# Full 64-row stacks of the k and q parts in the DRAM scratch of an attention and feed-forward block

## What is computed

```python
xn = layernorm(x)                                   # x: (8, 1024, 256)
u, v, q, k = split(silu(xn @ W1 + b1), 4)
scores = einsum('bqhd,bkhd->bhqk', q, k)            # 16 heads of 16 features
av = einsum('bhqk,bkhd->bqhd', silu(scores) / S, v)
attn = (layernorm(av * u) * gamma + beta) @ W2 + b2
h = gelu((layernorm(xn) * g1 + b1') @ ternary(w1).T + fb1)
ffn = (layernorm(h) * g2 + b2') @ ternary(w2).T + fb2
out = x + attn + ffn
```

## Time and profile before

| | |
|---|---|
| median of 3 runs | 1576.9 us |
| the profiled execution | 1573.26 us |
| its span, first to last instruction | 1571.5 us |
| mean granted PE clock | 0.985 of full speed |
| PE busy | 1473.2 us, 94% |
| ACT busy | 1207.9 us, 77% |
| DVE busy | 897.5 us, 57% |
| DMA queue of SP | 121.81 MB in 62192 packets |
| HBM read, written | 79.84 MB, 41.94 MB |

### The profile page before, as it was taken

One profiled execution on the slowest core, in us unless ns is written; L12 is line 12 of the kernel. 1 busy time (PEld: TensorE's weight loads), 2 busy tenths in 40 slices (PEclk: granted clock), 3 DMA queues, 4 the chain that ended last, 5 costly groups with the idle time before them and its releaser, 6 DMA issues.

```text
span 1571.5 us, 25337 instructions
## 1 busy us (share of the span) xinstructions
PE 1473.2 (94%) x9826; PEld 779.0 (50%) x9826; DVE 897.5 (57%) x1716; ACT 1207.9 (77%) x1269; POOL 101.4 (6%) x193
## 2 busy tenths in 40 slices
PE   4599999999999999999989999999999999999987
PEld 3245454545545555454545545455454555545434
DVE  4447644576546754476545764467554676447544
ACT  1378787887878888687878888788787888868783
POOL 2000100001000100001000010000100010000000
PEclk9699999999999999999999999999999999999999
DMA  4623116430345204352063311653034610535100
GB/s 151 147 67 69 55 33 143 117 84 5 78 109 134 55 15 112 90 108 55 14 148 89 73 55 33 143 122 79 2 74 114 135 54 14 114 88 108 28 1 28
DMA packets 62312, 123.43 MB, mean 79 GB/s; under 512 B 7664, under 2 KB 9328, under 8 KB 61168
## 3 DMA queue, kind: packets, MB, share of 16 engines
q1 hardware_dynamic: 62192, 121.81, 32.8%
HBM read 79.84 MB, written 41.94 MB: 77 GB/s over the span
## 4 chain that ended last, share of the span: by engine, by line
issue 66%; PE 22%; POOLq 4%; ACT 2%; DVE 2%; DMA 2%; POOL 1%; DVEq 0%; SPq 0%; ACTq 0%
PE outs L949 8%; PE scores L930 5%; POOLq L524 2%; PE fill L986 2%; PE fill L1020 2%; PE fill L1004 2%; ACT attn L557 2%; PE fill L1036 1%; PE fill L1013 1%; DMA KS<-k_scratch 1%; DMA q_scratch<-qst 1%; POOLq L516 1%; POOL rs L510 1%; POOLq L500 1%; PE fill L995 0%
## 5 line engine op out<-in xcount | busy, mean ns | idle before, releaser
L557 ACT ACTIVATE attn<-scores 128x1024 f32<-128x1024 f32 x1024 | 991.0, 1024 | 257.6 <-PE scores L930 253.7
L949 PE MATMUL outs<-attn,V 128*32 128x512 f32 x4096 | 499.6, 606 | 0.0
L930 PE MATMUL scores<-QS,KS 64*128 64x512 f32 x2048 | 395.6, 455 | 48.5 <-DMA KS<-k_scratch 24.4
L930 PEld LDWEIGHTS scores<-QS,KS 64*128 64x128 f32 x2048 | 165.0, 186 | 346.1 <-ACT attn L557 258.6
L949 PEld LDWEIGHTS outs<-attn,V 128*32 128x32 f32 x4096 | 108.0, 110 | 242.0 <-issue 241.8
L820 DVE TENSOR_TENSOR tmp<-fill,l2g 128x512 f32<-128x512 f32 x128 | 88.5, 691 | 112.3 <-PE fill L1013 105.6
L803 DVE SCALAR_TENSOR_TENSOR hid<-fill,ratq,fb1b 128x512 f32<-128x512 f32 x128 | 96.1, 751 | 66.3 <-PE fill L1004 62.9
L1020 PE MATMUL fill<-Wq,hgh 128*128 128x256 f32 x512 | 131.9, 295 | 1.9 <-DVE hgl L827 1.1
L986 PE MATMUL fill<-xp,W1h 128*128 128x512 f32 x384 | 126.6, 411 | 0.8 <-ACT qst L563 0.8
L1020 PE MATMUL fill<-Wq,hgl 128*128 128x256 f32 x512 | 125.0, 282 | 0.0
L1020 PEld LDWEIGHTS fill<-Wq,hgh 128*128 128x128 f32 x512 | 97.4, 190 | 22.4 <-issue 16.1
(11 more groups left out here) (110 smaller groups left out, 1358.9 us busy)
## 6 DMA issues: line engine op xcount, KB each, us to landing
QS<-q_scratch SPq DMA_DIRECT2D x128, 256.0 KB, 7.6
k_scratch<-kst SPq DMA_DIRECT2D x64, 256.0 KB
q_scratch<-qst SPq DMA_DIRECT2D x64, 256.0 KB
KS<-k_scratch SPq DMA_DIRECT2D x64, 256.0 KB, 4.3
KS<-k_scratch SPq DMA_DIRECT2D x128, 128.0 KB, 5.2
xin<-in_x SPq DMA_DIRECT2D x8, 1024.0 KB, 8.2
out_dram<-part SPq DMA_DIRECT2D x16, 512.0 KB, 2.6
w1raw<-in_W SPq DMA_DIRECT2D x1, 1024.0 KB, 7.1
```

Source lines behind the costliest of these rows:

```text
L557: nc.scalar.activation(attn_of(g)[:, 2 * hf:2 * hf + 2, :], SP[:, 2 * hf:2 * hf + 2, :], ACT.Silu).then_inc(s_silu, 1)
L930: ins = mm(SP[:, j, :], KS[rows, pair, t * P:(t + 1) * P], QS[rows, pair - c * PPC, h * HALF:(h + 1) * HALF], start=True, stop=True)
L949: ins = mm(OP[32 * j:32 * j + 32, g // RUN % 2, :], V[:, t, c * HPC // 2 + j, o * DH:o * DH + 2 * DH], attn_of(g)[:, n, :], start=(o == 0 ...
```

## The change

The scratch tensors get 64 rows per head in place of 32. `write_parts` writes the high part and the rest twice each, in the order in which the stack wants them: four transfers for k and four for q in place of two and two. `load_k` and `load_q` then need one transfer of 64 rows for each e: two in place of six, and two in place of four. The bytes that are loaded stay the same. The bytes that are written to scratch double, from 33.6 MB (128 transfers of 256 KB) to 67.1 MB. No other engine's instructions change.

```diff
+K_ROWS = (0, 1, 1, 0)
+Q_ROWS = (0, 1, 0, 1)
-WROTE = 16 * PARTS
-K_STACKED = 16 * 6
-Q_STACKED = 16 * 4
+WROTE = 16 * len(K_ROWS)
+K_STACKED = 16 * 2
+Q_STACKED = 16 * 2
...
-    kd = [nc.dram_tensor(f"k_scratch{c}", [HPC, QROWS, SEQ], F32, kind="Internal").ap() for c in range(DC)]
-    qd = [nc.dram_tensor(f"q_scratch{c}", [HPC, QROWS, SEQ], F32, kind="Internal").ap() for c in range(DC)]
+    kd = [nc.dram_tensor(f"k_scratch{c}", [HPC, TERMS, SEQ], F32, kind="Internal").ap() for c in range(DC)]
+    qd = [nc.dram_tensor(f"q_scratch{c}", [HPC, TERMS, SEQ], F32, kind="Internal").ap() for c in range(DC)]
...
                 sp.wait_ge(s_split, 8 * b + n + 1)
-                for r in range(PARTS):
-                    sp.dma_start(kd[c][:, r * DH:(r + 1) * DH, cols], kst[:, r, :].bitcast(F32)).then_inc(s_kw, 16)
+                for r, part_of in enumerate(K_ROWS):
+                    sp.dma_start(kd[c][:, r * DH:(r + 1) * DH, cols], kst[:, part_of, :].bitcast(F32)).then_inc(s_kw, 16)
                 sp.wait_ge(s_split, 8 * b + n + 2)
-                for r in range(PARTS):
-                    sp.dma_start(qd[c][:, r * DH:(r + 1) * DH, cols], qst[:, r, :].bitcast(F32)).then_inc(s_qw, 16)
+                for r, part_of in enumerate(Q_ROWS):
+                    sp.dma_start(qd[c][:, r * DH:(r + 1) * DH, cols], qst[:, part_of, :].bitcast(F32)).then_inc(s_qw, 16)
...
                 for e in range(2):
-                    for at_row, first, rows in ((0, 0, QROWS), (QROWS, DH, DH), (QROWS + DH, 0, DH)):
-                        sp.dma_start(KS[e * TERMS + at_row:e * TERMS + at_row + rows, pairs, cols].bitcast(F32),
-                                     kv[e, first:first + rows, :, cols]).then_inc(s_kst[c][h], 16)
+                    sp.dma_start(KS[e * TERMS:(e + 1) * TERMS, pairs, cols].bitcast(F32),
+                                 kv[e, :, :, cols]).then_inc(s_kst[c][h], 16)
...
                 for e in range(2):
-                    for at_row in (0, QROWS):
-                        sp.dma_start(QS[e * TERMS + at_row:e * TERMS + at_row + QROWS, :, cols].bitcast(F32),
-                                     qv[e, :, :, cols]).then_inc(s_qst[h], 16)
+                    sp.dma_start(QS[e * TERMS:(e + 1) * TERMS, :, cols].bitcast(F32),
+                                 qv[e, :, :, cols]).then_inc(s_qst[h], 16)
```

## The result

The changed kernel takes 1641.7 us, the kernel before 1578.7 us on the same chip (medians of four runs each). The ratio is 1.0398 with a 95% interval of 1.0362 to 1.0434: 4.0% slower, 63 us. The forecast was 1615.5 us in a range of 1595 to 1648, with 0.85 on slower. The sign and the place were right; the size was not, 63 us in place of 39.

A forecast was written before the change was run, and what follows sets the result against it. PE was taken to bound the kernel, waiting at group 8 on a queue of transfer bytes. 2.6 - 1.7 + 5.2 - 2.0 = +4.1 us in eight bodies, 32.8, plus 5.8 for the clock, gave 1615.5 us, range 1595 to 1648.

The forecast's parts named there:

- writes of h=1: Queue between the h=0 loads and the wait of `load_k`: four 256 KB writes become eight, 5.2 us more per body.
- the door: PE's wait at the scores of group 8 for the second half of `KS`: from 3.05 to about 7.1 us.
- KS load of h=1: Last load before group 8: 1.0 MB at 225 GB/s takes 4.7 us in place of 6.7, 2.0 us less.
- rival 3: Loads get no faster, 192 GB/s stays because of a DRAM-side limit: 1645 to 1656 us, chance 0.09.
- two more q writes for h=0: Writes before SP's KS load of h=0: 1.3 us each, 2.6 us more per body, bounds 1.2 and 3.7.
- loads of h=0: KS and QS loads, 2.1 MB in 64-row transfers at 225 GB/s: 9.3 us in place of 11.0, 1.7 less.
- Nothing gives it back: After group 8: PE's later work follows in the same order, so the +4.1 us per body stays.
- The wait at group 0: Sign of being wrong: a new PE wait for QS of more than a few us; first body's first group 0.9 later.
- The clock: PE at the 1.2 GHz level after all eight group 8 waits: four more at 1.44 us, 5.8 us, bounds 0 and 17.
- c=1 at nothing: Writes and loads for c=1 grow by 8 us but have some 40 us of cover until group 40: no cost.
- Rival 1: Tall loads run at 353 GB/s like those over 128 partitions: -1.0 us per body, 1563 us, chance 0.10.
- Rival 2: Loads at 300 to 335 GB/s, gain and cost cancel: time stays at 1572 to 1582 us, chance 0.05.

The follow-up runs named there:

- the run with parts innermost: Changed kernel with the scratch reordered so the copies of a feature lie side by side, two copies per write, against the kernel before: ratio 0.9853, 1558.9 us.
- the changed kernel with 16 engines: Changed kernel with W1 and b1 columns reordered so a write's slowest DRAM dimension is 16 features, not 8 heads, against the kernel before: ratio 0.9961, 1574.7 us.

## Why the prediction was right, and where its size was off

*Place and mechanism: right.* The queue works in the order of issue, the writes of h=1 stand between the loads and the next load, and the door is group 8. The wait for KS was to be 57 us in eight times; it is 52.1 in eight, and 67.9 with the part of it that is taken at group 0. SP's KS load of h=1 was to be issued 13.6 us after the split of `q.0.1`; it is issued 15.3 us after it (1224.2 and 1239.57).

*The range:* luck has a part in it. The forecast's own bounds were 1603 to 1636 us, and 1641.7 lies above them. It is inside 1595 to 1648 only because the range was stretched for rival 3, whose mechanism did not come true.

*The terms of the sum,* measured as the same spans in one body before and after:

| term | forecast | measured | from |
|---|---|---|---|
| two more q writes for h=0 | +2.6 | +3.5 | issue of q to issue of KS, 5.38 and 8.84 us |
| loads of h=0 | -1.7 | -0.9 | issue of KS to the end of full share, 12.3 and 11.4 us |
| writes of h=1 | +5.2 | +5.3 | from there to the KS issue, 5.5 and 10.8 us |
| KS load of h=1 | -2.0 | -1.0 | issue to scores, 8.75 and 7.77 us |
| sum | +4.1 | +6.9 | |

Over the seven bodies after the first the sum is 6.2 to 7.2 us, 6.6 on average. The rates were right, 217 to 229 GB/s for the loads and the half share for the writes. What was wrong is that I counted rates alone. *"I take 2.6, because the start is paid once either way"* fails: after two writes' worth of bytes the rate falls once more, to 113 GB/s from 1213.5 to 1214.5, though all four writes had been issued by 1211.9; why is open. *The step from 11.0 to 9.3 us* and *from 6.7 to 4.7 us* fail by 0.8 and 1.0 us. A part of it is the start of the 512 KB transfers: the KS load of h=1 moves bytes in earnest from 1.4 us after its issue on (1239.57, 1241.0), before the change from 0.8 us on (1185.70, 1186.5), and the rate in the middle of a stretch does not contain that. The whole span from issue to landing would have been the row to compare. Apart from this, the two spans that I took from the chain, 6.82 and 6.46 us, are to be read from the start of the last issue (1178.83 and 1187.94 in the earlier trace rows), not from its end.

*"Nothing gives it back"* held. *The wait at group 0* I had looked at only for the first body, and it is one of the signs that I named for being wrong: PE waits for QS, 15.8 us in seven bodies. It adds no term to the sum, because it is the same delay taken earlier on the same queue, with a wait at group 8 still behind it. That is why the wait for KS is 5 us below the forecast although the sum was too small. ACT's wait for `s_qw`, the other sign, came once as before, 7.9 us in place of 4.5.

*The clock:* the level and the place were right, all eight waits at group 8 have it, but the price was not. From the first scores to the transposes it is 1253.19 - 1247.34 = 5.85 us in the body shown, 2.67 us more than at the full level, and between 1.4 and 2.7 us more in the others; I had taken 1.44 us for each. In sum these stretches grew by about 10 us against the kernel before, where I had 5.8. PE's busy time grew by 15.0 us (bound 17), since in four bodies the low level also follows the wait at group 0, 1.4 to 1.7 us each. That part costs no time: PE only reaches its wait at group 8 later.

With the measured terms it closes: group 8 of the first body comes 5.1 us later (75.27 for 70.14), the queue in the seven others brings 46.3 us, together 51.4 where the forecast had 32.8. The rest to the 63.4 us of the span, 12 us, lies behind the waits at group 8, and about 10 us of it is the low clock.

*c=1 at nothing* held: no wait of PE for it appeared.

*Rival 1* was wrong for 64 rows; its rate comes with 128. *Rival 2* fell with it. *Rival 3* is as near the measured time (63 us against its 68 to 79) as the forecast's upper bound is, but its cause is not there: the loads did get faster, 192 to 217 GB/s.

## What to carry to other kernels

When transfers are merged, price the side that pays: here 33.6 MB of added writes went through eight of sixteen engines and stood ahead of the load that PE waits for. Look at the DMA busy share of a stretch before you count its bytes: here a share of 0.5 with a full queue was a layout to mend. Making the slowest dimension of the write in DRAM 16 in place of 8 gave 2.4% without the change and 4.4 points with it, and the tall loads by themselves 0.8%. Take the cost of one more transfer from a whole span, issue to landing, not from the rate inside a stretch. Ask of every wait that grows whether another wait on the same chain stands behind it; if so, the two are one cost. And add the low clock to the last of them.

## What was not expected of the hardware

- Four writes in a row are not four times one. SP's issue of the fourth takes 1.36 us in place of 0.57 (the expectation of the run with parts innermost calls it the third), and behind full loads the four q writes take SP 5.81 us. The rate of the data dips as well, to 113 GB/s for 1 us between the second and the third write.
- Writes on 16 engines end raggedly. In the changed kernel with 16 engines the share falls below 0.25 between 0.75 and 1.75 us before SP's next KS load at the seven later doors of group 8, with eight engines 0.5 to 1.0 us before it. Most of the longer gaps hold a share of 0.04 to 0.07, as much as one engine of sixteen that is not done; that it is one engine is inferred, and why it would lag is open.
- The length of a wait does not say alone whether the clock falls. In the changed kernel waits at group 0 of 2.67, 2.22, 2.02 and 2.28 us were followed by a mean clock of 0.66 to 0.67 over 5 us, and waits of 2.19, 2.16 and 2.25 us by the full clock. One of each (third number from the end):

```profile
256.50:261.50 5.00, 4.99 (x27) 1.68 (x27) 0.69 (x1) 2.33 (x3) 0.00 (x0) 0.67 0.53 203
1229.70:1234.70 5.00, 4.67 (x34) 2.02 (x34) 1.70 (x5) 3.91 (x5) 0.00 (x0) 1.00 0.53 204
```
